# A mixture-of-experts kernel on one core: half of each tile's normalisation moves from GpSimd to ScalarE

## The chip, the core and the metric

The kernel runs on one core of a Trainium2 chip. A core has five engines that run side by side and wait for one another on semaphores: TensorE (PE in the profile, with PEld for its weight loads), VectorE (DVE), ScalarE (ACT), GpSimd (POOL) and SyncE (SP). The metric is the device time of one execution in microseconds (us), as the median of several runs. Before the change it is 693.15 us, the median of three runs (691.65 to 693.29).

## What is computed

Input is x of 16 x 512 x 128 numbers in float32, so 8192 tokens of 128 values. Three residual steps follow one another:

```
x = x + 0.5 * ffn(layernorm(x))
x = x + attn(layernorm(x))
x = x + 0.5 * ffn(layernorm(x))
```

`ffn` is a mixture of eight experts, two for each token, without learnt routing:

```
h   = mod(int(x_flat[:, :2].sum(axis=1)), 8)
sel = [h, mod(h + 1, 8)]
y_e = maximum(x_flat @ W1[e] + b1[e], 0) @ W2[e] + b2[e]      # 128 -> 512 -> 128
out = sum over e in sel of 0.5 * y_e
```

`attn` is a gated linear recurrence over the 512 positions of each sequence. `layernorm` has no learnt scale; it subtracts the mean and divides by the root of the variance plus 1e-5.

## The kernel before

**Stages.** The program sorts the tokens by `h`, runs the first expert stage (`ffn(0)`, about 60 to 310 us of the span), then the recurrence, then sorts anew and runs the second expert stage (`ffn(1)`, about 430 to 685 us). Each engine has one program for the whole, written by hand, and the engines meet only on semaphores. The change touches the two expert stages alone.

**Tiles.** Since tokens of one `h` share both experts, the sorted tokens are cut into NJ = 39 tiles of FT = 256 rows, each in two halves (SUB = 2) of 128 rows, one row to a partition. A row in DRAM (`rows`) holds 128 values, and behind them the two numbers of its normalisation: the negative mean times the scale, in column D, and the scale, in column D + 1.

**What is done for a tile t.** POOL gathers the two halves with two indirect DMAs (L458) into `G`, of which there are four (SLOTS). POOL normalises both halves, `xn = G * scale + bias` over 127 columns (L478, `normalise`), into one of two `xn`; only the first two tiles of a stage are normalised by ACT (L589). PE transposes `xn` into PSUM (L768). ACT writes the high part of it as float16 (`x_high`, L583) and DVE the low part (`x_low`, L989). PE runs the first layer of each of the two experts e, 12 matmuls each (L732 to L734), ACT takes the high part of the positive side (`high`, L577), DVE the low one (`low`, L994), and PE runs the second layer, 16 matmuls for each expert (L750, L752). DVE has meanwhile written `O = G + b2` (`residual`, L1003) and adds the second layer's sums (`collect`, L1009 and L1012), and POOL scatters the two halves of `O` with two indirect DMAs (L465).

**Orders that matter.** Every engine works its queue strictly in the order of its program.
- PE in step t: first layer of expert 0 for tile t; then, after a wait for `xn_ready`, the transposes of tile t+1; second layer of expert 0 for tile t-1; first layer of expert 1 for t; second layer of expert 1 for t-1. A first layer waits for `low` of the same expert on the tile before, and for `x_low`.
- ACT for tile t: `high` of expert 0, `x_high` of t+1, `high` of expert 1.
- DVE for tile t: `low` of expert 0, `x_low` of t+1, `residual` of t, `low` of expert 1, `collect` of t-1.
- POOL in iteration j: two gathers for tile j+3 (after `res_done` of j-1, which frees the slot), first half of the normalisation of tile j+2, two scatters of tile j-2 (after `o_ready`), second half of the normalisation of j+2, which raises `xn_ready`. The normalisation waits for the gather to have landed (`gath`) and for the transposes of tile j to have read the same `xn` buffer (`xt_ready`).

## Time and profile before

| | us |
|---|---|
| median of three runs | 693.15 (691.65 to 693.29) |
| the profiled execution | 696.44 |
| its span, first to last instruction | 694.6 |
| PE busy | 578.8 (83%) |
| PE weight loads busy | 469.0 (68%) |
| DVE busy | 451.1 (65%) |
| POOL busy | 439.6 (63%) |
| ACT busy | 260.9 (38%) |

All durations below come from the one profiled execution. Its own time is 696.44 us, 1.8 us of it outside the span, and it is 3.3 us above the median of the runs. An engine's busy time is the sum of its instructions' durations without waits; matmuls overlap in the pipeline, so PE's busy time isn't its time at its peak. Of one instruction a timeline row gives the start and the duration and, in brackets, how long its engine was idle before it and which instruction of another engine ended the wait; "issue" is idle time without such a releaser, and "remote" means that none was found on this core.

### The profile page before, as it was taken

The numbers are of one execution on the slowest core, as the hardware profiler recorded it, in microseconds if no ns is written. First come the engines' busy times: TensorE is split into PE (matmuls) and PEld (weight loads), VectorE is DVE, ScalarE is ACT, GpSimd is POOL, SyncE is SP. The second block draws the span as 40 slices with busy tenths as digits, with TensorE's granted clock in tenths as the row PEclk, the third lists the DMA queues.
The fourth block names the chain that finished last, engine by engine and source line by source line (L and its number), as shares of the span: only waits on it lengthen the run. The fifth ranks groups of instructions, "written<-read, shape, count | busy, mean of one in ns | idle before, by whom it ended". The sixth has DMA issues, their size and how long they took to land.

```text
span 694.6 us, 15463 instructions
## 1 busy us (share of the span) xinstructions
PE 578.8 (83%) x5193; PEld 469.0 (68%) x5193; DVE 451.1 (65%) x1022; ACT 260.9 (38%) x378; POOL 439.6 (63%) x584
## 2 busy tenths in 40 slices
PE   0299999999999999976899479799999999999992
PEld 0155878877787778862566346687877877788781
DVE  6885766666666666666867684466676666666661
ACT  1455433434333333322886000333343333334340
POOL 2044778888888888740046402577778888888852
PEclk9998999999999999997999777999999999999997
DMA  9993111111111111209003530111111111221210
GB/s 241 329 189 47 44 39 44 43 44 44 43 42 39 40 34 37 43 11 241 2 1 80 106 62 15 30 42 43 45 40 47 43 43 44 43 44 30 33 24 0
DMA packets 46424, 41.87 MB, mean 60 GB/s; under 512 B 6485, under 2 KB 39595, under 8 KB 46354
## 3 DMA queue, kind: packets, MB, share of 16 engines
q1 hardware_dynamic: 35378, 21.65, 13.9%
q0 software_dynamic: 9984, 18.81, 11.4%
q8 instruction: 49, 0.80, 0.5%
q10 hardware_dynamic: 992, 0.44, 0.3%
q14 instruction: 21, 0.17, 0.1%
HBM read 23.93 MB, written 18.74 MB: 61 GB/s over the span
## 4 chain that ended last, share of the span: by engine, by line
PE 31%; DVE 18%; POOL 18%; issue 14%; ACT 8%; another core or an unknown queue 6%; DMA 2%; SPq 2%; POOLq 0%; DVEq 0%; ACTq 0%
PE ps L750 6%; POOL G L458 6%; DVE hlo L994 5%; ACT hhi L577 5%; POOL x1d L465 4%; PE ps L734 4%; PE ps L732 4%; POOL xn L478 4%; PE ps L733 3%; PE ps L752 3%; POOL out L465 3%; PE ps L714 3%; DVE O L1012 2%; SPq L343 2%
## 5 line engine op out<-in xcount | busy, mean ns | idle before, releaser
L994 DVE SCALAR_TENSOR_TENSOR hlo<-ps,hhi 128x1024 f16<-128x1024 f32 x156 | 190.9, 1224 | 165.2 <-ACT hhi L577 119.7
L577 ACT ACTIVATE hhi<-ps 128x1024 f16<-128x1024 f32 x156 | 159.8, 1025 | 296.8 <-PE ps L734 255.8
L750 PE MATMUL ps<-w2s,hhi 128*128 x1248 | 222.7, 273 | 0.2 <-issue 0.2
L752 PE MATMUL ps<-w2s,hlo 128*128 x1248 | 214.3, 219 | 0.2 <-issue 0.2
L458 POOL DMA_INDIRECT G<-rows,places x156 | 157.3, 1009 | 86.9 <-DVE places L960 43.4
L732 PE MATMUL ps<-xhi,w1s 128*128 128x256 f16 x624 | 170.8, 274 | 9.7 <-DVE xlo L989 6.1
L733 PE MATMUL ps<-xlo,w1s 128*128 128x256 f16 x624 | 170.7, 274 | 0.1
L734 PE MATMUL ps<-xhi,w1s 128*128 128x256 f16 x624 | 170.7, 274 | 0.0
L750 PEld LDWEIGHTS ps<-w2s,hhi 128*128 128x128 f16 x1248 | 122.2, 98 | 13.7 <-issue 0.3
L752 PEld LDWEIGHTS ps<-w2s,hlo 128*128 128x128 f16 x1248 | 122.2, 98 | 2.4 <-issue 0.5
L465 POOL DMA_INDIRECT out<-O,places x78 | 80.0, 1026 | 32.4 <-issue 18.0
L465 POOL DMA_INDIRECT x1d<-O,places x78 | 80.0, 1026 | 29.8 <-issue 18.2
L478 POOL TENSOR_SCALAR xn<-G 128x127 f32<-128x127 f32 x148 | 83.0, 561 | 4.2
L732 PEld LDWEIGHTS ps<-xhi,w1s 128*128 x624 | 61.1, 98 | 21.4 <-issue 14.0
L734 PEld LDWEIGHTS ps<-xhi,w1s 128*128 x624 | 61.2, 98 | 7.9 <-issue 0.3
L733 PEld LDWEIGHTS ps<-xlo,w1s 128*128 x624 | 61.2, 98 | 5.5 <-issue 0.3
L768 PE MATMUL ps<-ident,xn 128*128 128x128 f32 x156 | 33.5, 296 | 31.8 <-POOL xn L478 30.3
L768 PEld LDWEIGHTS ps<-ident,xn 128*128 128x128 f32 x156 | 16.8, 142 | 49.5 <-POOL xn L478 48.3
L664 PE MATMUL ps<-ones_row,ones 128*128 128x512 f16 x133 | 39.3, 460 | 10.4 <-DMA X<-x1d 9.7
L1009 DVE SCALAR_TENSOR_TENSOR O<-ps,scl_i,O 128x256 f32<-128x256 f32 x78 | 37.1, 475 | 3.8 <-PE ps L752 3.8
L1012 DVE SCALAR_TENSOR_TENSOR O<-ps,scl_i,O 128x256 f32<-128x256 f32 x78 | 37.7, 484 | 2.8
L1003 DVE TENSOR_TENSOR O<-G,b2t 128x128 f32<-128x128 f32 x156 | 38.6, 288 | 0.0
(217 smaller groups left out, 519.4 us busy)
## 6 DMA issues: line engine op xcount, KB each, us to landing
rows<-X SPq DMA_DIRECT2D x2, 2080.0 KB, 21.5
rows<-X SPq DMA_DIRECT2D x4, 1040.0 KB, 7.4
X<-in_L_attn_x SPq DMA_DIRECT2D x8, 512.0 KB, 7.3
X<-x1d SPq DMA_DIRECT2D x8, 512.0 KB, 7.4
G<-rows,places POOLq DMA_INDIRECT x156
w1r<-in_L_ffn_W SPq DMA_DIRECT2D x1, 2048.0 KB, 11.0
x1d<-O,places POOLq DMA_INDIRECT x78
out<-O,places POOLq DMA_INDIRECT x78
```

What stands on the lines that cost most here:

```text
L458: nc.gpsimd.indirect_dma_start(out=G[tile.slot][:, s, :], out_offset=None, in_=rows, in_offset=bass.IndirectOffsetOnAxis(ap=idx[:, s:s + 1 ...
L465: nc.gpsimd.indirect_dma_start(out=dst, out_offset=bass.IndirectOffsetOnAxis(ap=idx[:, SUB + s:SUB + s + 1], axis=0), in_=O[tile.slot][:, ...
L478: ins = g.tensor_scalar(xn[tile.k][:, s, 0:D - 1], a[:, 0:D - 1], a[:, D + 1:D + 2], a[:, D:D + 1], ALU.mult, ALU.add)
L577: nc.scalar.activation(hhi[tile.k][e][:], H[e], ACT.Relu).then_inc(hi_done[e], 1)
L732: nc.tensor.matmul(o, hi, xhi[tile.k][:], start=True, stop=False)
L733: nc.tensor.matmul(o, hi, xlo[tile.k][:], start=False, stop=False)
L734: ins = nc.tensor.matmul(o, lo, xhi[tile.k][:], start=False, stop=True)
L750: nc.tensor.matmul(Y[tile.k][:, s, :], hhi[tile.k][e][:, c, tok], w, start=first, stop=False, skip_group_check=True)
L752: ins = nc.tensor.matmul(Y[tile.k][:, s, 0:P], hlo[tile.k][e][:, c, tok], wh, start=False, stop=(e == 1 and c == CH - 1), skip_group_check ...
L768: ins = nc.tensor.transpose(XTP[:, s * P:(s + 1) * P], xn[(tile + 1).k][:, s, :], ident[:])
L994: v.scalar_tensor_tensor(out=hlo[tile.k][e][:], in0=H[e], scalar=0.0, in1=hhi[tile.k][e][:], op0=ALU.max, op1=ALU.subtract).then_inc(lo_do ...
L1012: v.scalar_tensor_tensor(out=o, in0=Y[tile.k][:, :, P:2 * P], scalar=scl[:, 2:3], in1=o, op0=ALU.mult, op1=ALU.add).then_inc(o_ready, 1)
```

## The change

POOL no longer normalises the first half of a tile. In an iteration it gathers, scatters, and then normalises the second half, which raises `xn_ready` as before. ACT gets a function `normalise_half`: it waits for the gather of tile t+2 and for the transposes of tile t, computes the first half with one activation, and raises a new semaphore, `xn_act`. It stands between `x_high` of tile t+1 and the second `high` of tile t. PE waits for `xn_act` too before it transposes a tile from the third on. The first two tiles of a stage go as before.

```diff
+            def shared(self):
+
+                return self.r * (NJ - 2) + self.j - 1
...
-                def normalise(tile, s):
-
-                    a = G[tile.slot][:, s, :]
-                    if s == 0:
-                        pool.wait_ge(gath[tile.slot], tile.moved())
-                        pool.wait_ge(xt_ready, (tile + -2).done())
-                        if tile.j == 2:
-                            pool.wait_ge(xn_ready, (tile + -1).done())
-                    ins = g.tensor_scalar(xn[tile.k][:, s, 0:D - 1], a[:, 0:D - 1], a[:, D + 1:D + 2], a[:, D:D + 1], ALU.mult,
-                                          ALU.add)
-                    if s == SUB - 1:
-                        ins.then_inc(xn_ready, 1)
+                def normalise(tile):
+
+                    a, s = G[tile.slot][:, 1, :], 1
+                    pool.wait_ge(gath[tile.slot], tile.moved())
+                    pool.wait_ge(xt_ready, (tile + -2).done())
+                    if tile.j == 2:
+                        pool.wait_ge(xn_ready, (tile + -1).done())
+                    g.tensor_scalar(xn[tile.k][:, s, 0:D - 1], a[:, 0:D - 1], a[:, D + 1:D + 2], a[:, D:D + 1], ALU.mult,
+                                    ALU.add).then_inc(xn_ready, 1)
...
-                    if j + 2 < NJ:
-                        normalise(tile + 2, 0)
                     if j >= BEHIND:
                         pool.wait_ge(o_ready, (tile + -BEHIND).done())
                         scatter(tile + -BEHIND, idx)
                     if j + 2 < NJ:
-                        normalise(tile + 2, 1)
+                        normalise(tile + 2)
...
+                def normalise_half(tile):
+                    g = G[tile.slot]
+                    act.wait_ge(gath[tile.slot], tile.moved())
+                    act.wait_ge(xt_ready, (tile + -2).done())
+                    nc.scalar.activation(xn[tile.k][:, 0, 0:D - 1], g[:, 0, 0:D - 1], ACT.Identity,
+                                         bias=g[:, 0, D:D + 1], scale=g[:, 0, D + 1:D + 2]).then_inc(xn_act, 1)
...
                     high(tile, 0)
                     if j + 1 < NJ:
                         x_high(tile + 1)
+                    if j + 2 < NJ:
+                        normalise_half(tile + 2)
                     high(tile, 1)
...
                         pe.wait_ge(xn_ready, (tile + 1).done())
+                        if tile.j >= 1:
+                            pe.wait_ge(xn_act, (tile + 1).shared())
```

## Rows read from the trace of the kernel before

**Rows 1.** windows view: length, busy us (instructions) by engine, clock, DMA share
```profile
101.42:288.82 187.40, 170.95 (x1744) 149.31 (x1742) 121.67 (x211) 69.72 (x90) 157.04 (x181) 1.00 0.18 41
449.48:523.53 74.05, 68.63 (x698) 59.46 (x697) 48.74 (x85) 27.55 (x36) 57.57 (x69) 1.00 0.16 43
523.53:660.97 137.44, 125.36 (x1280) 109.46 (x1278) 89.22 (x155) 51.12 (x66) 115.21 (x133) 1.00 0.19 41
```

**Rows 2.** page, costliest groups: busy us, mean ns | idle before, and what ended it
```profile
L768 PEld LDWEIGHTS ps<-ident,xn 128*128 128x128 f32 x156 | 16.8, 142 | 49.5 <-POOL xn L478 48.3
```

**Rows 3.** timeline, POOL, one steady tile: start, us, line, [idle before]
```profile
203.50 1.02 POOL L458 DMA_INDIRECT G<-rows,places  x1 [0.17 <-DVE O L1012]
204.83 0.96 POOL L458 DMA_INDIRECT G<-rows,places  x1 [0.30 <-issue]
205.83 0.70 POOL L478 TENSOR_SCALAR xn<-G 128x127 f32<-128x127 f32 x1
206.70 1.06 POOL L465 DMA_INDIRECT x1d<-O,places  x1 [0.17 <-issue]
208.07 1.00 POOL L465 DMA_INDIRECT x1d<-O,places  x1 [0.31 <-issue]
209.09 0.48 POOL L478 TENSOR_SCALAR xn<-G 128x127 f32<-128x127 f32 x1
```

**Rows 4.** timeline, PE, steady tile
```profile
203.39 0.33 PE L768 MATMUL ps<-ident,xn 128*128 128x128 f32 x1 [0.57 <-POOL xn L478]
...
204.98 0.27 PE L732 MATMUL ps<-xhi,w1s 128*128 128x256 f16 x1
...
206.18 0.27 PE L734 MATMUL ps<-xhi,w1s 128*128 128x256 f16 x1
```

**Rows 5.** timeline, PE, first layers of the last two tiles of a stage
```profile
295.06 0.27 PE L732 MATMUL ps<-xhi,w1s 128*128 128x256 f16 x1
...
300.53 0.27 PE L732 MATMUL ps<-xhi,w1s 128*128 128x256 f16 x1
```

**Rows 6.** timeline, PE, first layers that bound the other pattern (with rows 1)
```profile
77.59 0.27 PE L732 MATMUL ps<-xhi,w1s 128*128 128x256 f16 x1
...
467.16 0.28 PE L732 MATMUL ps<-xhi,w1s 128*128 128x256 f16 x1 [0.48 <-DVE xlo L989]
...
486.24 0.28 PE L732 MATMUL ps<-xhi,w1s 128*128 128x256 f16 x1 [0.48 <-DVE xlo L989]
```

**Rows 7.** timeline, POOL, in the other pattern
```profile
458.45 1.06 POOL L465 DMA_INDIRECT out<-O,places  x1 [0.18 <-issue]
...
465.38 1.06 POOL L465 DMA_INDIRECT out<-O,places  x1 [1.08 <-DVE O L1012]
```

**Rows 8.** timeline, PE, in the other pattern
```profile
459.01 0.27 PE L734 MATMUL ps<-xhi,w1s 128*128 128x256 f16 x1
...
463.87 0.28 PE L732 MATMUL ps<-xhi,w1s 128*128 128x256 f16 x1 [0.43 <-DVE hlo L994]
```

**Rows 9.** timeline, ACT, in the other pattern
```profile
461.35 1.02 ACT L577 ACTIVATE hhi<-ps 128x1024 f16<-128x1024 f32 x1 [3.59 <-remote]
```

**Rows 10.** timeline, DVE, steady and in the other pattern
```profile
205.79 0.48 DVE L1003 TENSOR_TENSOR O<-G,b2t 128x128 f32<-128x128 f32 x2
...
459.00 0.48 DVE L1003 TENSOR_TENSOR O<-G,b2t 128x128 f32<-128x128 f32 x2
```

**Rows 11.** timeline, ACT, steady tile
```profile
204.19 0.38 ACT L583 ACTIVATE xhi<-ps 128x256 f16<-128x256 f32 x1
206.49 1.03 ACT L577 ACTIVATE hhi<-ps 128x1024 f16<-128x1024 f32 x1 [1.93 <-PE ps L734]
```

**Rows 12.** one tile's instructions (xn) by line, and timeline, ACT, stage start
```profile
L589 ACT ACTIVATE xn<-G x8: 478/486/493, 63.5 to 435.0; 128x127 f32<-128x127 f32 x8
...
63.47 0.88 ACT L589 ACTIVATE xn<-G 128x127 f32<-128x127 f32 x2
```

**Rows 13.** timeline, POOL, stage start
```profile
60.95 0.95 POOL L458 DMA_INDIRECT G<-rows,places  x1 [0.31 <-issue]
```

More of the change, by code:

```diff
@@ L228, in macaron_kernel @@
         xn_ready = sem("xn_ready")
+        xn_act = sem("xn_act")
         xt_ready = sem("xt_ready")
```

## The prediction

> **What bounds the kernel now.** I read the windows view first [rows 1]. The two expert stages hold most of the span, and in them TensorE is granted its full clock, the DMA engines are idle over four fifths of the time, and POOL is as busy as it gets in this kernel (157.04 of 187.40 us), while ACT works 69.72 us. In the page's groups one row of TensorE names POOL: the weight loads of the transposes (L768) have 49.5 us of idle time before them, 48.3 of it for `xn` of POOL's L478 [rows 2]. So the next view is POOL's timeline over one tile [rows 3]. It has no slack: gather 1.02, gap 0.30, gather 0.96, gap 0.04, first normalisation 0.70, gap 0.17, scatter 1.06, gap 0.31, scatter 1.00, gap 0.02, second normalisation 0.48, gap 0.17. Together 6.23 us; tile follows tile each 6.24 to 6.25 us (187.40 us for 30 tiles, 137.44 us for 22 [rows 1]). The gap put down to DVE's `O` is the same 0.17 as the one put down to issue, so it is no wait. POOL's own work is the period.
>
> TensorE is close behind. It stands for 0.57 us until POOL's second normalisation is done and transposes at 203.39, just before POOL's next gather [rows 3, 4]. What it would need alone is shown by the last tiles of a stage, where POOL has only scatters left: two first layers start at 295.06 and 300.53 us, 5.47 us apart [rows 5].
>
> **A second pattern in the same stages.** Not all tiles go so. Four periods of the first stage (77.59 to 101.42 us, 5.96 each) and twelve of the second (449.48 to 523.53 us, 6.17 each) differ [rows 1, 6]. There POOL isn't the period: at 465.38 it has waited 1.08 us for `O` [rows 7]. The late one is ACT: the first layer's last matmul (L734) starts at 459.01 and ends by 459.28 [rows 8], and ACT, idle for 3.59 us, starts on it at 461.35, 2.07 us later, its idle time being put down to "remote" [rows 9]. The delay goes on through DVE's `hlo` to TensorE, which stands until 463.87, 2.52 us after ACT's start [rows 8]. In the steady pattern ACT follows the same layer by 0.04 us (206.18 + 0.27 = 206.45, ACT at 206.49) [rows 4, 11]. No row says what holds this completion back. I take it that it comes where TensorE runs without waiting for `xn` while gathers and scatters are issued densely; the end of the stage, with scatters alone, has a period of 5.47 and so no such delay [rows 5].
>
> **The change part by part.**
> - POOL loses the first normalisation of each tile from the third on. In the steady pattern 0.04 + 0.70 + 0.17 go and a gap of 0.30 between two indirect DMAs (as between the gathers) comes: 0.61 less, a loop of 6.23 - 0.61 = 5.62 us [rows 3]. The waits for the gather and for the transposes two tiles back stay, now behind the scatters; no row shows either as a wait.
> - ACT gets one activation of 128x127 a tile. The same shape (L589) takes 486 ns [rows 12]. It is put behind `x_high`: 204.19 + 0.38 = 204.57 to 205.06, and the next thing queued is the second `high`, at 206.49 [rows 11]. With the period shortened by 0.61 it comes at about 205.9, as the idle transposing time is what goes. So 0.49 us costs nothing; without that cover (when the first `high` comes so late that the second stands behind it) it would delay the second `high` by up to 0.49 us, and DVE's `low` and the next first layer of TensorE wait for that.
> - The added wait on ACT is for the gather of tile t+2. Queued behind it is the second `high`. The last issue of a gather ends at 204.83 + 0.96 = 205.79 [rows 3], and ACT asks for it a tile later, at 204.57 + 6.24 = 210.81, 5.0 us on. The landing that rows bound ends at most 63.47 - 60.95 = 2.5 us after its issue started: ACT uses the first gathered tile then [rows 12, 13]. So this wait is free, and would be with a landing of twice that time. The wait for the transposes of tile t is a whole tile old.
> - TensorE's second wait, for ACT's half, is over 4 us before the transposes (205.06 against 203.39 + 6.24 = 209.63). Cost 0.
> - The scatters and the gathers behind them move up in the loop. No scatter of the steady pattern waits for `O`, and none of the rows shows a wait for their landing: cost 0 while POOL is the period, and where it isn't, POOL waits for `O` as it did at 465.38 [rows 7], which is free too.
>
> Sum for the steady pattern: the period goes from 6.25 to the larger of 5.62 (POOL) and 5.47 (TensorE): 0.63 us for each of 52 periods, 32.6 us. If all 68 periods got to 5.62, the other 16 (23.83 + 74.05 = 97.9 us, 6.12 each) would give another 8.0.
>
> **Where I choose.** The steady pattern has TensorE recover 6.25 - 5.47 = 0.78 us a tile after a disturbance. With the change it has 0.15. The pattern with the late completions took 4 and 12 tiles to end with the larger reserve; with a fifth of it I expect it to come back for about half of the 52 periods. In it, POOL's shorter loop gives nothing by itself, since POOL waited there already. So half the steady periods get 0.63 (16.4 us) and half go at the mean of the late pattern, 6.12, in place of 6.25 (3.4 us); the 16 stay. Sum 19.8 us. From the profiled execution (696.44 us, span 694.6) that is 676.6; the median of the three runs is 693.15, 3.3 below it, and so 673.3, which I round to 673. The bounds for this case are a fifth and nine tenths of the periods in the clean loop: 0.2 x 32.6 + 0.8 x 6.8 = 12.0 and 0.9 x 32.6 + 0.1 x 6.8 = 30.0, so 663 to 681, widened to 689 by the 0.49 us that ACT's added work could cost on late tiles (some 16 of them, 8 us).
>
> **The rivals.**
> - Clean loop throughout: POOL's 5.62 everywhere. For it: TensorE's 5.47 at the stage's end with ACT on time; against it: the reserve of 0.15. 32.6 + 8.0 = 40.6 us: 652.5. Chance 0.22, over 648 to 663.
> - No change, the late pattern nearly everywhere: 691 to 695. The late pattern's longest part repeats over three tiles in 19.08 us (467.16 to 486.24 [rows 6]), 6.36 each, beside parts of 5.96, so that its mean can well be that of now. Chance 0.10.
> - DVE holds POOL up. At 205.83 the first normalisation takes 0.70, the second 0.48; only the first lies beside DVE's residual add (L1003, 205.79 to 206.27) [rows 3, 10]. Without it the add falls on gathers or scatters. If it held one for its whole 0.48 us, the loop would be 6.10, and 52 periods would give 7.8 us: 685.4. Against it: at 459.00 the same add lies inside the scatter of 458.45, and that takes 1.06, as the one of 206.70 does beside none [rows 3, 7, 10]. Chance 0.05, within 683 to 691. The Trainium skill, GPSIMD Engine Reference, section Key points, says that GpSimd shares its SBUF interfaces with VectorE and contends with its instructions of two SBUF inputs, which the add is. By that rule the indirect DMAs would be held too; the row at 458.45 doesn't bear it out.
> - Slower: ACT is late on every tile. From the transposes to the end of the second expert's first layer are 206.45 - 203.39 = 3.06 us; then comes the lateness, and 2.52 from ACT's start to TensorE's; and that layer starts 204.98 - 203.39 = 1.59 after its own step's transposes [rows 4, 8]. The period is then at least 3.06 + 2.52 - 1.59 = 3.99 plus the lateness, and beats 6.25 if that exceeds 2.26 us. Denser indirect DMAs on POOL speak for it, the mean of 6.12 that the late pattern has now speaks against it. At 6.36 over all 68 periods it is 68 x 6.36 - 422.7 = 9.8 us more: 703. Chance 0.23.
> - That ACT's half isn't ready (it waits for the gather and holds the second `high`) I give under 0.02, in the slower part.
>
> **How the numbers follow.** Forecast (663 to 689) 0.40, clean 0.22, DVE holding POOL 0.05, no change 0.10, slower 0.23. The likeliest is 673. For 8 times in 10 the range takes in the clean loop and most of the slower case: 650 to 701; below lies some 0.06, above some 0.08. A difference under 0.3% (2.1 us) can't be told from none; by these cases faster has 0.67, same 0.10, slower 0.23.
>
> **What would show it.** POOL's timeline: 0.30 us between the second gather and the first scatter, and a period of 5.62 where nothing else holds. `xn` by ACT at about 0.49 us, with no DMA as releaser. The waits of L768 for L478 shrink from 0.57 to about 0.1 us a tile, and the next wait is TensorE's for `hlo` or `xlo`. The half-and-half case shows ACT's `hhi` 2 us or more behind L734 on many tiles and POOL waiting for `O`; if ACT is on time everywhere and the periods are 5.6, the clean rival holds. I am wrong altogether if POOL's DMAs get longer than 1.06, if ACT's half shows a wait for G, or if the first layers come more than 6.25 us apart.

## The result and the profile after

The change makes the kernel slower: 732.84 us (729.99 to 733.99) against 693.22 us for the kernel before in the same comparison, a ratio of 1.056 (95% interval 1.052 to 1.061). The profiled execution took 733.1 us, with a span of 731.4 us; it lies 0.3 us from the median, so what its trace shows isn't an effect of taking it.

The page's costliest groups, and the longest rows of the waits view (engine, line, what it waited for: us in total, times, longest):

```profile
L577 ACT ACTIVATE hhi<-ps 128x1024 f16<-128x1024 f32 x156 | 159.2, 1023 | 307.5 <-remote 211.7
L463 POOL DMA_INDIRECT G<-rows,places x156 | 157.4, 1009 | 84.6 <-DVE places L971 39.7
L470 POOL DMA_INDIRECT out<-O,places x78 | 79.5, 1019 | 78.1 <-DVE O L1023 60.4
L779 PE MATMUL ps<-ident,xn 128*128 128x128 f32 x156 | 34.2, 290 | 12.4 <-POOL xn L482 8.3
L597 ACT ACTIVATE xn<-G 128x127 f32<-128x127 f32 x74 | 36.5, 493 | 2.1 <-DMA G<-rows,places 2.1
L482 POOL TENSOR_SCALAR xn<-G 128x127 f32<-128x127 f32 x74 | 36.2, 489 | 1.8
```
```profile
ACT hhi L577 <- remote: 211.7, 66, 6.0
DVE hlo L1005 <- ACT hhi L577: 160.0, 97, 5.7
POOL out L470 <- DVE O L1023: 60.4, 21, 4.8
POOL x1d L470 <- DVE O L1023: 56.5, 21, 4.4
```

ACT's half costs what it should (493 ns, waiting 2.1 us in all for a gather), POOL's work has fallen, and TensorE hardly waits for `xn` any more. What has grown is the number of ACT's waits ahead of `hhi` that the view puts down to "remote": 66 with 211.7 us, where the kernel before had 15 with 40.9 us. The same two rows of the kernel before:

```profile
L577 ACT ACTIVATE hhi<-ps 128x1024 f16<-128x1024 f32 x156 | 159.8, 1025 | 296.8 <-PE ps L734 255.8
ACT hhi L577 <- remote: 40.9, 15, 4.2
```

The row counts the whole idle time of such a wait, also the part in which TensorE was still at the layer. ACT's idle time ahead of `hhi` has grown in all from 296.8 to 307.5 us only, so the 211.7 us are no loss by themselves; what the row tells is how many waits ended by an event that came late. Such a stretch in timelines of ACT, PE and POOL:

```profile
204.31 1.02 ACT L577 ACTIVATE hhi<-ps 128x1024 f16<-128x1024 f32 x1 [1.78 <-PE ps L743]
205.23 0.38 ACT L583 ACTIVATE xhi<-ps 128x256 f16<-128x256 f32 x1
205.50 0.49 ACT L597 ACTIVATE xn<-G 128x127 f32<-128x127 f32 x1
210.96 1.02 ACT L577 ACTIVATE hhi<-ps 128x1024 f16<-128x1024 f32 x1 [4.97 <-remote]
213.29 1.02 ACT L577 ACTIVATE hhi<-ps 128x1024 f16<-128x1024 f32 x1 [1.31 <-remote]
```
```profile
202.63 0.27 PE L741 MATMUL ps<-xhi,w1s 128*128 128x256 f16 x1
...
205.97 0.27 PE L741 MATMUL ps<-xhi,w1s 128*128 128x256 f16 x1
...
207.18 0.27 PE L743 MATMUL ps<-xhi,w1s 128*128 128x256 f16 x1
208.60 0.27 PE L741 MATMUL ps<-xhi,w1s 128*128 128x256 f16 x1
...
213.53 0.28 PE L741 MATMUL ps<-xhi,w1s 128*128 128x256 f16 x1
216.17 0.27 PE L741 MATMUL ps<-xhi,w1s 128*128 128x256 f16 x1
```
```profile
204.50 1.02 POOL L463 DMA_INDIRECT G<-rows,places  x1 [0.18 <-issue]
205.83 0.96 POOL L463 DMA_INDIRECT G<-rows,places  x1 [0.30 <-issue]
207.09 1.13 POOL L470 DMA_INDIRECT x1d<-O,places  x1 [0.30 <-issue]
208.52 1.00 POOL L470 DMA_INDIRECT x1d<-O,places  x1 [0.30 <-issue]
209.54 0.49 POOL L482 TENSOR_SCALAR xn<-G 128x127 f32<-128x127 f32 x1
210.21 1.02 POOL L463 DMA_INDIRECT G<-rows,places  x1 [0.17 <-issue]
211.54 0.96 POOL L463 DMA_INDIRECT G<-rows,places  x1 [0.30 <-issue]
214.98 1.02 POOL L470 DMA_INDIRECT x1d<-O,places  x1 [2.49 <-DVE O L1023]
```

The second expert's first layer ends at 207.18 + 0.27 = 207.45; ACT, idle, starts on it at 210.96, 3.51 us later. This is the late completion of [rows 8, 9], there 2.07 us. It has become the rule: in the rows above tiles go in pairs, 202.63 to 208.60 to 216.17, 5.97 and 7.57 us, 6.77 on average. TensorE runs on meanwhile (its next layer starts at 208.60), so it is the event that is late, not the matmuls. The same holds one layer on: ACT is idle for 1.31 us before it starts at 213.29. POOL now waits for `O` (2.49 us at 214.98).

Where the time went, by the windows view of 32 tiles of each stage, first of the kernel before, then of the changed one (length; busy us of PE, PEld, DVE, ACT, POOL; clock; DMA share; GB/s):

```profile
83.07:282.56 199.49, 182.77 (x1858) 159.29 (x1857) 129.72 (x225) 74.36 (x96) 165.68 (x191) 1.00 0.17 41
454.96:654.71 199.75, 182.82 (x1859) 158.90 (x1858) 129.84 (x225) 74.02 (x96) 163.92 (x191) 1.00 0.17 42
```
```profile
80.88:298.08 217.20, 194.27 (x1859) 157.48 (x1857) 128.97 (x224) 86.06 (x128) 144.07 (x160) 1.00 0.16 38
470.70:690.85 220.15, 193.69 (x1859) 157.73 (x1857) 129.27 (x225) 86.07 (x128) 143.23 (x160) 1.00 0.16 38
```

217.20 + 220.15 against 199.49 + 199.75 is 38.1 us more; the spans differ by 731.4 - 694.6 = 36.8. A tile takes 6.79 and 6.88 us in place of 6.23 and 6.24. The granted clock is full in all four stretches: here the clock plays no part.

### The profile page after: what moved, and what is told of

It reads as the page before. It is cut to its first block, busy times and chain, and to the rows that moved or that the text cites. A ratio compares the mean times of both kernels' runs of the same rounds, so it can differ in the third digit from the quotient of the medians.

```text
span 731.4 us, 15537 instructions
## 1 busy us (share of the span) xinstructions
PE 600.1 (82%) x5193; PEld 465.2 (64%) x5193; DVE 449.7 (61%) x1022; ACT 288.0 (39%) x452; POOL 391.6 (54%) x510
## 3 DMA queue, kind: packets, MB, share of 16 engines
q0 software_dynamic: 9984, 18.81, 10.9%
## 4 chain that ended last, share of the span: by engine, by line
PE 27%; DVE 18%; issue 17%; another core or an unknown queue 15%; ACT 9%; POOL 8%; DMA 2%; SPq 1%; POOLq 0%; DVEq 0%; ACTq 0%
PE ps L759 5%; DVE hlo L1005 5%; ACT hhi L577 5%; PE ps L741 3%; PE ps L743 3%; PE ps L761 3%; PE ps L742 3%; POOL x1d L470 3%; PE ps L723 3%; POOL out L470 3%; PE ps L779 2%; DVE O L1023 2%; PE ps L673 2%; POOL xn L482 2%
## 5 line engine op out<-in xcount | busy, mean ns | idle before, releaser
L577 ACT ACTIVATE hhi<-ps 128x1024 f16<-128x1024 f32 x156 | 159.2, 1023 | 307.5 <-remote 211.7
L759 PE MATMUL ps<-w2s,hhi 128*128 x1248 | 231.9, 273 | 11.8 <-issue 10.5
L761 PE MATMUL ps<-w2s,hlo 128*128 x1248 | 219.3, 219 | 7.5 <-issue 4.8
L463 POOL DMA_INDIRECT G<-rows,places x156 | 157.4, 1009 | 84.6 <-DVE places L971 39.7
L470 POOL DMA_INDIRECT out<-O,places x78 | 79.5, 1019 | 78.1 <-DVE O L1023 60.4
L470 POOL DMA_INDIRECT x1d<-O,places x78 | 79.5, 1019 | 74.0 <-DVE O L1023 56.5
L597 ACT ACTIVATE xn<-G 128x127 f32<-128x127 f32 x74 | 36.5, 493 | 2.1 <-DMA G<-rows,places 2.1
L482 POOL TENSOR_SCALAR xn<-G 128x127 f32<-128x127 f32 x74 | 36.2, 489 | 1.8
```

Source lines behind the costliest of these rows:

```text
L463: nc.gpsimd.indirect_dma_start(out=G[tile.slot][:, s, :], out_offset=None, in_=rows, in_offset=bass.IndirectOffsetOnAxis(ap=idx[:, s:s + 1 ...
L470: nc.gpsimd.indirect_dma_start(out=dst, out_offset=bass.IndirectOffsetOnAxis(ap=idx[:, SUB + s:SUB + s + 1], axis=0), in_=O[tile.slot][:, ...
L482: g.tensor_scalar(xn[tile.k][:, s, 0:D - 1], a[:, 0:D - 1], a[:, D + 1:D + 2], a[:, D:D + 1], ALU.mult, ALU.add).then_inc(xn_ready, 1)
L577: nc.scalar.activation(hhi[tile.k][e][:], H[e], ACT.Relu).then_inc(hi_done[e], 1)
L759: nc.tensor.matmul(Y[tile.k][:, s, :], hhi[tile.k][e][:, c, tok], w, start=first, stop=False, skip_group_check=True)
L761: ins = nc.tensor.matmul(Y[tile.k][:, s, 0:P], hlo[tile.k][e][:, c, tok], wh, start=False, stop=(e == 1 and c == CH - 1), skip_group_check ...
```

## The experiments

They ran on several chips. In the comparison above and in one of those below the kernel before takes 693 to 694 us, in four others, on four other chips, 719 to 722; no trace of it exists from the second kind. So each run is given as a ratio to the kernel before on its own chip. For the same reason the changed kernel itself was run twice more (e5, e16).

All runs in one table. "ACT, remote" is the waits row of `hhi` with releaser "remote" (us, times); "PE for xn" the times that TensorE's transposes waited for POOL's normalised half, of 74 tiles; "tile" the mean distance of 32 tiles' first layers in the first stage. A wait is "remote" in these views only when the event came some 1.5 us or more behind the end of its matmul (the smallest such lateness in any run's timeline is 1.53 us); smaller ones are counted with the layer itself. "Late event" below means such a wait.

```
run                    before, us  ratio [95%]            ACT, remote   PE for xn  tile, us
before                 693         1                       40.9 us  15     58       6.23
changed                693         1.056 [1.052, 1.061]   211.7     66     32       6.79
e5  changed            694         1.052 [1.048, 1.056]   209.7     64     28       6.73
e16 changed            722         1.102 [1.092, 1.111]   236.7     40     26       7.89
e1  order              722         0.999 [0.995, 1.003]   211.5     62     11       6.61
e11 order              720         1.002 [0.998, 1.005]   220.8     66     10       6.63
e2  pace               722         1.010 [1.005, 1.016]   174.6     52     38       6.75
e3  own wait           722         no interval            161.5     28      0       7.75
e4  no half            722         1.092 [1.080, 1.104]   236.8     39     26       7.74
e6  scatters plain     694         0.910 [0.906, 0.914]     4.1      1      1       5.48
e7  no indirect DMA    694         0.897 [0.894, 0.901]     0        0      0       5.48
e8  fixed experts      694         1.000 [0.997, 1.003]   142.9     49      5       6.25
e9  half between       720         1.047 [1.039, 1.056]   199.7     53      1       7.50
e10 locked             720         0.995 [0.992, 0.998]   200.2     54      1       6.65
e12 before, locked     720         1.036 [1.030, 1.043]     0        0     71       6.94
e13 later scatter      722         1.137 [1.129, 1.146]   255.8     55      2       7.93
e14 third half         722         0.988 [0.979, 0.996]     4.3      1     65       6.46
e15 pads               722         0.991 [0.983, 0.998]   175.5     60     33       6.53
e17 more matmuls       719         1.079 [1.069, 1.089]   152.2     30      0       7.32
e18 small pad          719         0.974 [0.967, 0.981]    19.1      7     61       6.39
```

### First: order, pace, ACT

e1 moves POOL's first half behind the scatters, in the kernel before.

```diff
-                    if j + 2 < NJ:
-                        normalise(tile + 2, 0)
                     if j >= BEHIND:
...
                     if j + 2 < NJ:
+                        normalise(tile + 2, 0)
                         normalise(tile + 2, 1)
```

> The kernel before with one change: POOL normalises both halves behind its scatters. ACT does nothing new. POOL's loop keeps all its work (about 6.2 us a tile). If the order alone were the cause of the loss, this gets near the changed kernel's 733 us. If the cause is that POOL's loop is too short to hold TensorE back (late completions), this stays at 693, give or take 5, with ACT at most 0.5 us behind L734 on most tiles. If ACT's added activation is the cause, it stays at 693 too.

720.04 us, 0.999. The order alone changes nothing in the time. But ACT has 62 late events, against the expectation that it follows the layer by at most 0.5 us on most tiles. Whether the order or the chip did that stays open, since there is no trace of the kernel before from this kind of chip: its 27 us more over 74 tiles are 0.36 us, which with 6.23 makes an estimate of 6.6 us a tile, what e1 has (6.61). So it may well have had as many late events.

e2 is the changed kernel, and POOL computes the first half too, into scratch, between gathers and scatters.

```diff
+                    if j + 2 < NJ:
+                        t2 = tile + 2
+                        a = G[t2.slot][:, 0, :]
+                        pool.wait_ge(gath[t2.slot], t2.moved())
+                        pool.wait_ge(xt_ready, tile.done())
+                        g.tensor_scalar(scr[t2.k][:, 0:D - 1], a[:, 0:D - 1], a[:, D + 1:D + 2], a[:, D:D + 1], ALU.mult, ALU.add)
                     if j >= BEHIND:
```

> The changed kernel, with POOL also computing the first half into a scratch tile that nobody reads, at its old place before the scatters. So POOL has the length of before and ACT has its new activation. If the late completions come from POOL no longer pacing TensorE, this returns to about 693 us (688 to 698). If ACT's activation (and the wait in front of it) is the cause, it stays at 725 or more.

729.0 us, 1.010. Beside e16 (1.102 on the same kind of chip) work without use on POOL takes nine tenths of the loss away, though 52 events are still late.

e3 lets TensorE wait, ahead of the transposes, for the end of its own first layer.

```diff
                             pe.wait_ge(xlo_ready, tile.done())
+                            pe.wait_ge(h_ready[0], tile.done())
```

> The changed kernel, with one more wait: TensorE waits for the completion of its own first layer of expert 0 (h_ready) before it transposes the next tile, so it can't run on without a stop. If completions come late because TensorE runs on, they come in time here and the period is near POOL's 5.6 to 5.8 us: 650 to 670 us. If they come late whatever TensorE does, the wait only adds to it: 735 us or more.

763 to 784 us in four executions, too far apart for a ratio: 6 to 9% over the kernel before. That is no cure, though not worse than the changed kernel on such a chip either (e16, 1.102). The run tells one thing more. TensorE's own wait, for its own event, is late five times:

```profile
PE ps L780 <- remote: 10.9, 5, 3.6
```

So the delay doesn't lie in how ScalarE takes the event up.

e4 takes POOL's first half out of the kernel before and gives it to nobody: `xn`'s first half keeps the values of the first two tiles, the output differs.

```diff
-                    if j + 2 < NJ:
-                        normalise(tile + 2, 0)
...
-                    if s == 0:
+                    if s == 1:
                         pool.wait_ge(gath[tile.slot], tile.moved())
```

> The kernel before without POOL's first half of the normalisation from the third tile of a stage on; nobody computes it, so those rows of xn keep the values of an earlier tile. ACT does nothing new. If the shorter POOL loop is the cause, this is as slow as the changed kernel, 725 to 740 us, with ACT 2 us and more behind L734. If ACT's activation is the cause, this gains what the sum said: 650 to 675 us.

787.58 us (two executions), 1.092. ACT's added activation is not the cause: without it, and without POOL's half, the kernel loses about as much as the changed one on such a chip (1.102).

### Second: whose is the late event

e5 is the changed kernel unaltered.

> The changed kernel itself, unaltered, so that the next runs have it beside them on the same chip. Two theories of the loss. A: the events that TensorE's finished matmuls send come late while GpSimd is at its indirect DMAs, and the changed spacing of these DMAs makes it worse. B: the work that ScalarE got makes it late, and everything behind it. Neither says anything of this run but that the loss is there again: 4 to 7% over the kernel before on the same chip if a chip that runs the kernel before at 720 us loses as the one at 693 us did; if the ratio is near 1.01, the loss is a matter of the chip, and the run in which GpSimd kept both halves' work explained nothing.

1.052: as in the first comparison.

e6 lets SyncE write the tiles with plain DMAs, in the order of the tiles, so that the output's rows are in another order; POOL keeps its wait for `O` and computes on scratch twice.

```diff
-                        nc.gpsimd.indirect_dma_start(
-                            out=dst, out_offset=bass.IndirectOffsetOnAxis(ap=idx[:, SUB + s:SUB + s + 1], axis=0),
-                            in_=O[tile.slot][:, s, :], in_offset=None,
-                            bounds_check=N - 1, oob_is_err=False).then_inc(scat[tile.slot], 16)
+                        g.tensor_scalar(scr[tile.j % 4 * 2 + s][:], scr[16][:], 1.0, 0.0, ALU.mult, ALU.add)
...
+                            sp.dma_start(dst[r0:r0 + P, :], O[t2.slot][:, s, :]).then_inc(scat[t2.slot], 16)
```

> The changed kernel, but the scatters are plain DMAs from SyncE to rows in order of the tiles (the output's rows are in another order), and GpSimd does two computations on scratch in their place, behind the same wait. The gathers stay on GpSimd. Theory A (the late events belong to GpSimd's indirect DMAs): half of these are gone, the waits of ScalarE for TensorE's events (211.7 us in the changed kernel) fall to under 110 us, and the time falls by 5 to 10%, towards the 650 us that TensorE's 5.47 us a tile would give. Theory B (ScalarE's added work): no change, within 1% of the changed kernel. Theory C (it is GpSimd's pace and its waits, not its DMAs): no change either if the computations are as long as the scatters were.

631.8 us, 0.910: more than the 5 to 10% that theory A gave. e7 does the same with the gathers, of rows in order; POOL issues no DMA in the stages.

```diff
-                        nc.gpsimd.indirect_dma_start(
-                            out=G[tile.slot][:, s, :], out_offset=None, in_=rows,
-                            in_offset=bass.IndirectOffsetOnAxis(ap=idx[:, s:s + 1], axis=0)).then_inc(gath[tile.slot], 16)
+                        g.tensor_scalar(scr[8 + tile.j % 4 * 2 + s][:], scr[16][:], 1.0, 0.0, ALU.mult, ALU.add)
...
+                        sp.dma_start(G[tile.slot][:, s, :], rows[r0:r0 + P, :]).then_inc(gath[tile.slot], 16)
```

> As the run before, and the gathers too are plain DMAs from SyncE (of rows in order, so that the tokens are other ones), with two computations on scratch in their place on GpSimd, which then issues no DMA at all in the loops. Theory A: no late event is left; ScalarE waits for TensorE under 50 us in all, the first layers lie 5.47 us apart, and the time is 640 to 665 us. Theories B and C: ScalarE's waits stay above 150 us and the time stays within 2% of the changed kernel.

622.82 us, 0.897, below the 640 to 665 of theory A. The group of `hhi` on the page of e6 and of e7, and for e6 the scratch computation that stands where the scatters stood:

```profile
L589 ACT ACTIVATE hhi<-ps 128x1024 f16<-128x1024 f32 x156 | 159.7, 1024 | 214.6 <-PE ps L755 210.4
L485 POOL TENSOR_SCALAR scr<-scr 128x256 f16<-128x256 f16 x156 | 61.1, 411 | 60.0 <-DVE O L1035 40.8
```
```profile
L599 ACT ACTIVATE hhi<-ps 128x1024 f16<-128x1024 f32 x156 | 159.8, 1025 | 213.2 <-PE ps L765 213.2
```

ACT's idle time is now put down to the layer it waits for, all but 4.1 us in e6, and a tile takes 5.48 us, TensorE's own pace [rows 5]. The same bytes go in and out of the same buffers. With POOL at no indirect DMA no event is late, and without the scatters hardly one: the late events belong to POOL's indirect DMAs. One reservation: a scratch computation took 411 ns, not the scatter's 1019, so POOL is also less busy; against its mere busy time as the cause speak e2 and e14, where more of it helps. And the plain DMAs differ in more than the engine that issues them: they move rows in order, not scattered ones.

e8 gives TensorE fixed experts: the table isn't read, no address comes from a register (the output differs).

```diff
-                        hi = w1v[:, bass.ds(held[tile.j][e] + c * P, P)]
+                        hi = w1v[:, e * WS + c * P:e * WS + c * P + P]
...
-                    if 0 <= j < NJ:
-                        held[j] = load(j)
                     step(Tile(r, j))
```

> The changed kernel, but TensorE uses experts 0 and 1 for every tile (the output differs), with no table read and no address from a register in its loop. Theory A: no change, within 1% of the changed kernel, ScalarE's waits for TensorE stay near 210 us. Theory D (TensorE's own stream holds its events back: its register loads and addresses worked out at run time): the waits fall under 60 us and the time to 640 to 670 us.

694.0 us, 1.000, which is 5% below e5 on the same chip. Neither theory had this: 49 events are still late, and yet the whole loss is gone. So TensorE's register work isn't what makes events late, but without it the changed kernel is back at the time of the kernel before (which still has it). Why, the account below doesn't explain, and it wasn't taken further.

### Third: rows of DMAs, locks

e9 is the changed kernel with POOL's half between gathers and scatters (`normalise(tile + 2)` moved up), so that two indirect DMAs stand in a row and not four.

> The changed kernel, but GpSimd's remaining half stands between its two gathers and its two scatters, where the first half stood before, instead of behind the scatters. The work of every engine is that of the changed kernel; only the row of four indirect DMAs is cut into two rows of two. Theory A1: a TensorE event that falls due while GpSimd is at back to back indirect DMAs comes only some 0.6 us after the row's end, so a row of four holds it up to 4 us and a row of two at most about 2.5. Then this kernel is faster than the changed one by 5 to 9%, between 665 and 690 us where the kernel before takes 693, and ScalarE's waits marked remote fall from 210 us to under 60. Rival A2: only the number of indirect DMAs in a time counts, and the loop that has become shorter brings them closer: then it stays within 2% of the changed kernel, near 725 us.

753.93 us, 1.047: no cure, with 53 late events, though with less than half the loss of e16 (1.102, on another chip of the kind). e11 is e1 again, which makes rows of four in the kernel before.

> The kernel before with both halves on GpSimd behind its scatters, once more, since the chip of the first time ran the kernel before itself 4% slower than here. Theory A1: its row of four indirect DMAs makes it slower than the kernel before, by 3 to 8%, with ScalarE's waits marked remote above 120 us (40.9 us in the kernel before). Rival A2: the loop is as long as before, so nothing changes, within 0.5%, as the first time.

720.71 us, 1.002. The two together refute theory A1, by which e9 had to be faster than the kernel before and e11 slower: the length of a row of indirect DMAs isn't all that counts. That it is part of it, e9 leaves open.

e10 adds two waits to e9; e12 adds the same two to the kernel before.

```diff
                         if j >= 1:
                             pool.wait_ge(res_done, (tile + -1).done())
+                        pool.wait_ge(h_ready[0], tile.done())
                         gather(tile + AHEAD, idx)
...
                         pool.wait_ge(o_ready, (tile + -BEHIND).done())
+                        if j < NJ:
+                            pool.wait_ge(h_ready[1], tile.done())
                         scatter(tile + -BEHIND, idx)
```

> As the run before, and GpSimd also starts its two gathers only after the event of the first expert's first layer of the tile (h_ready[0]), and its two scatters only after that of the second expert's (h_ready[1]), so that no row of indirect DMAs runs when one of these two events falls due. Theory A1: the two events that ScalarE waits for are on time on nearly every tile, TensorE sets the pace, and the time is 625 to 655 us where the kernel before takes 693. Rival A2: no better than the run before, and slower by the added waits, 690 to 740 us.

> The kernel before, with nothing on ScalarE, but with the two waits of the locked run: gathers after h_ready[0], scatters after h_ready[1] of the tile. GpSimd's work of 5.3 us a tile (two gathers, a half, two scatters, a half) fits just into the 5.47 us of TensorE. Theory A1: the late events go here too, 640 to 670 us where the kernel before takes 693, and what the locked run with ScalarE's half gains beyond this one is what the change itself is worth: 5 to 15 us. Rival A2: 693 us or slower, since waits are only added.

e10: 715.31 us, 0.995, with as many late events as without the waits (54 and 53), and yet 5% faster than e9 on the same chip. Waits added to POOL thus take the loss away as computing does. e12: 743.88 us, 1.036, and not one late event. Its waits view:

```profile
ACT hhi L580 <- PE ps L737: 287.0, 150, 3.4
PE ps L771 <- POOL xn L478: 88.5, 71, 2.9
```

Here POOL waits for TensorE and TensorE for POOL, one behind the other; the tile is 6.94 us long from waiting, and yet all events are on time. The same two waits with POOL's loop shorter by one half's normalisation (e10) leave 54 late ones. What differs in the view is the second row: in e12 TensorE is held by POOL's `xn` on 71 tiles, in e10 on one.

### Fourth: why less work on POOL is worse

e13 scatters a tile one turn later (`AHEAD, BEHIND = 3, 3`).

> The changed kernel, but GpSimd scatters each tile one turn later (three tiles behind its gathers' loop instead of two), so that it hardly waits for VectorE's result O any more (117 us in the changed kernel). Theory P (the loss comes since GpSimd, no longer the slowest, starts its scatters when VectorE lets it, and so at times tied to TensorE's events): the waits of ScalarE marked remote fall from 210 us to under 80, and the time is at or below the kernel before's, ratio 0.94 to 1.00. Theory D (the loss comes since less of GpSimd's own computing lies between its indirect DMAs, whatever it waits for): no help, ratio to the kernel before 1.03 to 1.08, remote waits about 200 us.

816.67 us, 1.137, the slowest of all. The wait for `O` is gone from the scatters, but POOL waits elsewhere instead, at the gathers, for DVE's residual add:

```profile
ACT hhi L577 <- remote: 255.8, 55, 8.6
POOL G L463 <- DVE O L1014: 177.7, 44, 6.0
POOL out L470 <- DVE O L1023: 13.0, 5, 4.4
```

So the run says that the wait for `O` isn't the cause, not that waiting for DVE in general isn't; e6 says more on that, where POOL waits 118.8 us at its gathers (68 times) and all is well.

e14 adds a third half to the kernel before, into scratch (as in e2); e15 adds three small computations (128x64) to the changed kernel, so that no two indirect DMAs follow each other.

> The kernel before, and GpSimd computes a third half, into scratch, between its gathers and its scatters: one more step of GpSimd's computing a tile, after 0.5 us (the changed kernel, 5 to 5.6% slower) and 1.2 us (the kernel before). GpSimd's loop is then 6.8 us a tile and sets the pace. Theory D: the late events nearly vanish, ScalarE's remote waits are under 40 us, and the time is what the loop gives, 52 steady tiles by 0.55 us more: ratio 1.03 to 1.05. Theory P: as many late events as in the kernel before on the same chip, ratio 1.03 or more too; it is the remote waits that tell, and the shape of the curve.

> The changed kernel with three small computations on scratch (128 x 64), one behind the first gather, one behind the second, one behind the first scatter, so that no two indirect DMAs are back to back. GpSimd's loop is again about as long as in the kernel before. Theory D: the loss goes, ratio to the kernel before 0.97 to 1.02. Theory P: about the same, since GpSimd is again the slowest and waits for nobody: this run tests both against a third one, that the cause is the computation that was moved and not the time it took, by which the ratio stays at 1.05.

> The changed kernel itself, beside the other three. On a chip that runs the kernel before at 693 us its ratio was 1.052 to 1.056. If this chip is one of those at 720 us, the ratio says what there was to be undone in the runs made on such chips: 1.04 to 1.06 is expected by either theory, since the runs with half the computing were 1.047 and 1.092 there.

e16, the changed kernel: 791.78 us, 1.102, above the 1.04 to 1.06 expected. On this kind of chip the change costs twice as much. e15: 711.6 us, 0.991, so the whole loss is gone, on the same chip and with more late events than e16 has. The two rows show that the number doesn't set the time; the single wait is shorter:

```profile
ACT hhi L577 <- remote: 236.7, 40, 7.2
ACT hhi L584 <- remote: 175.5, 60, 4.4
```

That is 5.9 us a wait in e16 and 2.9 in e15. By the timelines, these events came on average 4.8 us behind their matmuls in e16 (4.8 in e4), 3.1 in the changed kernel of the first comparison, and 2.6 to 2.7 in e15, e1, e11, e8 and e10, which all take about the time of the kernel before (e2, at 1.010, is the exception with 3.1). Nor is the granted clock full where most is lost: between 80 and 290 us and between 480 and 680 us it is 0.97 and 0.98 in e16, 0.92 and 0.97 in e9, 0.92 and 0.90 in e13, but 1.00 and 1.00 in e1, e2 and e18. What that costs wasn't taken apart.

e14: 709.7 us, 0.988: the kernel before gets faster by work of no use. Its loop is 6.46 us and not the 6.8 expected; the first normalisation, where it no longer lies beside DVE's add, takes 0.47 in place of 0.70 (502 ns on average over both halves, 561 before), so that the 0.45 added cost 0.22. One event is late; smaller delays remain, as at 205.16 + 0.27 = 205.43, on which ACT starts at 206.11:

```profile
ACT hhi L583 <- PE ps L740: 276.7, 141, 3.3
PE ps L774 <- POOL xn L479: 54.2, 65, 1.6
ACT hhi L583 <- remote: 4.3, 1, 4.3
```

e17 gives TensorE 0.86 us more per tile in the changed kernel, by a matmul whose result the next one overwrites:

```diff
+                        nc.tensor.matmul(o, hi, xhi[tile.k][:], start=True, stop=True)
                         nc.tensor.matmul(o, hi, xhi[tile.k][:], start=True, stop=False)
```

> The changed kernel, with one matmul more before each of the first layers' accumulations: its result is overwritten, so the output stays the same, and TensorE has 8 more of 0.107 us pitch, 0.86 us a tile (5.47 to 6.33). The tiles, and with them GpSimd's indirect DMAs, then lie as far apart as in the kernel before, but TensorE and not GpSimd sets the pace, and GpSimd has no computing added. Theory D (only how close the indirect DMAs lie in time counts): the late events go, the time is that of 6.33 us a tile, near the kernel before's, and this kernel with more work is faster than the changed one: ratio to the kernel before 0.98 to 1.02. Theory L (the late events are few only where TensorE is held every tile by GpSimd's normalised half and so keeps a harmless place in GpSimd's loop): they stay, with remote waits of ScalarE near 200 us, and 0.86 us on 78 tiles come on top: ratio 1.08 to 1.2.

778.27 us, 1.079, just under the lower end of what theory L gave (1.08) and far from D's 0.98 to 1.02. The tiles lie 7.32 us apart, further than in the kernel before, and 30 events are late all the same:

```profile
ACT hhi L577 <- PE ps L744: 192.9, 113, 3.7
ACT hhi L577 <- remote: 152.2, 30, 6.6
```

How densely POOL issues indirect DMAs over a tile is therefore not all. (It is also no slower than e16, against an expected addition; the two ran on different chips.)

e18 adds one small computation (128x64, 0.23 us) between gathers and scatters of the kernel before.

```diff
+                    if j + 2 < NJ:
+                        g.tensor_scalar(scr[tile.j % 4][:], scr[4][:], 1.0, 0.0, ALU.mult, ALU.add)
                     if j >= BEHIND:
```

> The kernel before with a small computation on scratch (128 x 64, 0.27 us) between gathers and scatters, the dose between the kernel before and the run with a third half: GpSimd's loop 6.5 us. Theory L: TensorE is held by GpSimd on more tiles than in the kernel before, the late events fall to near nothing as with the third half, and the time is what the loop gives: on a chip that runs the kernel before at 720 us ratio 0.95 to 0.985, better than the third half's 0.9875, on one at 693 us 1.01 to 1.02. Theory D gives the same sign but a gradual fall of the late events: 0.98 to 1.0 on the first kind of chip.

701.14 us, 0.974 [0.967, 0.981], the fastest kernel of the study on a chip of this kind among those that leave nothing of the computation out; it was not run on one where the kernel before takes 693 us, and at 6.39 us a tile should not gain there. Its waits view has seven late events:

```profile
PE ps L772 <- POOL xn L480: 43.5, 61, 1.6
ACT hhi L581 <- remote: 19.1, 7, 4.2
```

### What they say together

Shown: without indirect DMAs on POOL no event of TensorE is late (e7), with the gathers alone one is (e6), and in both the tile takes 5.48 us. ACT's added work isn't the cause: with POOL's half simply left out about as much is lost (e4). So what costs is the work taken from POOL, and work or waits given back to it undo it: from 1.102 to 1.010 and 0.991 by computing (e2, e15), from 1.047 to 0.995 by waits (e9, e10); in the kernel before, computing gives 0.988 and 0.974 (e14, e18). The order on POOL doesn't change the time (e1, e11). The number of indirect DMAs in a row (e9, e11), the scatters' wait for `O` (e13) and the density of indirect DMAs (e17) are each not enough to explain it alone.

Not shown is by which path the missing work costs the time. The number of late events doesn't tell it: e15, e1 and e8 have 49 to 62 of them at 0.991 to 1.000. How late the single event comes goes with the loss better, if not strictly, from 2.6 to 4.8 us; what makes that difference no run isolates.

The table has one regularity that fits every run with four indirect DMAs a tile: where TensorE is held by POOL's `xn` on 58 tiles or more, 0 to 15 waits of ACT are "remote" (before, e12, e14, e18); where on 38 or fewer, 28 to 66 are. I read it so, and this part is argued: POOL's indirect DMAs delay those events of TensorE that fall due at certain places of POOL's loop. As long as POOL is the slowest and TensorE waits for its half, each first layer ends at the same, harmless place. Once POOL is the faster one, TensorE's events fall anywhere in its loop, some come 2 to 4 us late, and by ACT, DVE and TensorE's next layer each such delay lengthens the tile. e12 beside e10 and e14, e18 beside the rest support it; but late events also keep TensorE from waiting for POOL, so the regularity could arise the other way round, and e8, which loses nothing with 49 late events, doesn't fit the last step. What in the chip holds the event, and why the second kind of chip is worse (the kernel before may have lost its place there: e1 equals it with 62 late events), stays open.

## Why the prediction was wrong

673 us with 650 to 701 was forecast, 732.8 came: wrong in direction and outside the range. By its own steps:

- POOL's loop, 5.62 us: right where POOL doesn't wait. The gap between gather and scatter is the 0.30 foreseen, and from gather to gather 204.50 to 210.21 are 5.71 us, 0.07 of it a longer scatter.
- ACT's half, 0.49 us at no cost: right (0.493, and 2.1 us of waits for `G`). e4, which has no such half and loses about as much, agrees.
- TensorE's waits for `xn`: foreseen to shrink from 0.57 us to about 0.1, and they did ([rows 4]; 8.3 us in 32 waits now, 0.11 over 74 tiles). This was counted as the gain. By the reading above, which is argued, it was the loss of what kept the events on time.
- DVE holding POOL's DMAs for the add's whole 0.48 us: didn't happen. A gather takes 1009 ns on the page after, a scatter 1019. The first scatter of the rows above took 1.13 us with DVE's add (206.84 to 207.32) beside its start, the one at 214.98, with the next add (215.82) only at its end, 1.02; so at most some 0.1 us of it can be the add's. Beside a normalisation the same add does show: 0.70 us [rows 3], 0.47 where it lay apart in e14. The Trainium skill (GPSIMD Engine Reference, Key points) states that GpSimd contends with VectorE's instructions of two SBUF inputs; this case's rows agree for the normalisations, and hardly show it for the indirect DMAs.
- The step that failed is the one under "Where I choose". It saw the late completions and that they come where TensorE runs free of `xn`. But it priced them with what they cost in the kernel before: half the tiles at a mean of 6.12 us. There were 66 of them on 78 tiles, through both stages, and the tiles took 6.79 and 6.88 us on average; of the 0.63 us a tile that half the steady tiles were to gain (16.4 us), nothing came. The mean of 6.12 was measured where such stretches are short and end again in the steady pattern; in the changed kernel the steady pattern didn't come back. That a reserve of 0.15 us would still end half of them had no row behind it.
- The slower rival had the right mechanism with the wrong size. Its formula holds to 0.06 us: 3.99 + 3.51 of lateness is 7.50, and the second expert's first layers lie 213.53 - 205.97 = 7.56 apart. It put in a lateness of about 2.4, from a period of 6.36 of the kernel before, where in the rows above 3.51 comes on every second tile, followed by a short one of 5.97. At 0.23 its chance was too small, since the only argument against it was that same mean of 6.12; and its 703 us, at 6.36 a tile, lack the 0.4 to 0.5 us a tile that make the rest.
- Of the three signs of being wrong altogether the last came in full, first layers more than 6.25 us apart; the other two barely, a scatter of 1.13 us in place of 1.06 and ACT's 2.1 us of waits for `G`.

## What to carry to other kernels

If a trace shows completions of one engine that come late only while another issues indirect DMAs, price them as they could become in every tile, not as they are now, and ask what keeps the others on time: here it was, as far as the runs tell, the very wait that the change took away. Relieving the engine that sets the pace may be worth less than moving its indirect DMAs elsewhere; with the scatters off GpSimd, and their rows written in order, the kernel came to 5.48 us a tile (e6). Where that can't be done, a small computation on the pacing engine is a cheap probe (and was worth 2.6% on the one chip where e18 ran).

## What the runs showed of the hardware

TensorE's matmuls run on while the event of a finished one reaches ACT up to several us late (3.51 us in the rows above); TensorE itself sees its own event late too (e3, five waits of 10.9 us together). It happens in every kernel with four indirect DMAs a tile on GpSimd but e12, and not at all in the one with none. The kernel before takes 693 to 694 us on two occasions and 719 to 722 us on four other chips, and the change costs 5 to 6% on the ones and 10% on the one of the others where it was run.
